# State-space scan of a decoder: which engine makes the C products, and when the next round is prepared

## The reference

```python
h = _rms(x, norm_w[i])
xz = jnp.einsum('bld,ed->ble', h, W_in[i])
xi, z = jnp.split(xz, 2, axis=-1)
xc = _silu(conv_b[i] + sum((xp[:, k:k + L, :] * conv_w[i][:, k] for k in range(dc))))
delta, Bm, Cm = jnp.split(jnp.einsum('bld,ed->ble', xc, W_x[i]), [rk, rk + n], axis=-1)
delta = jax.nn.softplus(jnp.einsum('blr,dr->bld', delta, W_dt[i]) + b_dt[i])
deltaA = jnp.exp(delta[..., None] * A)
BX = (delta * xc)[..., None] * Bm[:, :, None, :]
_, hs = jax.lax.associative_scan(combine, (deltaA, BX), axis=1)
y = jnp.einsum('bldn,bln->bld', hs, Cm) + D[i] * xc
x = x + jnp.einsum('bld,ed->ble', y * _silu(z), W_out[i])
```

## Time and profile before

| what | value |
|---|---|
| median of 3 runs | 1598.68 us (1598.49 to 1600.09) |
| the profiled execution: its time, its span | 1598.81 us, 1597.1 us |
| busy over the span: PE / DVE / ACT / POOL | 1211.0 / 1111.4 / 753.1 / 857.8 us |
| the selective state-space units on VectorE | from 423.95 us to about 1248 us |
| scans with the C product behind them (L1468) | 160, 1821 ns each |
| scans with the C product on GpSimd (L1472) | 96, 1808 ns each |
| C products on VectorE (L1470) / on GpSimd (L1409) | 160 of 991 ns / 48 of 3571 ns |
| mean granted TensorE clock | 0.864 |

### The profile page before, as it was taken

One profiled execution on the slowest core, in us unless ns is written; L12 is line 12 of the kernel. 1 busy time (PEld: TensorE's weight loads), 2 busy tenths in 40 slices (PEclk: granted clock), 3 DMA queues, 4 the chain that ended last, 5 costly groups with the idle time before them and its releaser, 6 DMA issues.

```text
span 1597.1 us, 17149 instructions
## 1 busy us (share of the span) xinstructions
PE 1211.0 (76%) x5882; PEld 697.4 (44%) x5882; DVE 1111.4 (70%) x1630; ACT 753.1 (47%) x1692; POOL 857.8 (54%) x744
## 2 busy tenths in 40 slices
PE   6688888774568778787886868877777777788765
PEld 3454554442234444444443435444343445545444
DVE  3766767753487987879878888797888245554448
ACT  1454544533465455554555545545543144444553
POOL 5500010010587797778977879779787234343413
PEclk9898999987778888888998979888988789898976
DMA  6000010000502304014040050220400300000000
GB/s 183 20 10 10 10 60 1 1 1 0 204 1 84 118 0 166 14 43 160 0 152 27 2 200 1 100 80 1 165 1 1 93 26 15 14 14 1 2 1 21
DMA packets 21028, 79.88 MB, mean 50 GB/s; under 512 B 4273, under 2 KB 7417, under 8 KB 19961
## 3 DMA queue, kind: packets, MB, share of 16 engines
q1 hardware_dynamic: 20942, 78.79, 14.1%
HBM read 77.55 MB, written 1.23 MB: 49 GB/s over the span
## 4 chain that ended last, share of the span: by engine, by line
DVE 32%; PE 31%; POOL 15%; ACT 11%; issue 9%; DMA 1%; SPq 0%; DVEq 0%; ACTq 0%; POOLq 0%
PE ps L484 29%; DVE ps L1468 9%; POOL arena L1409 6%; POOL arena L1398 6%; DVE arena L1472 4%; DVE arena L1470 4%; DVE hstat L867 3%; ACT arena L691 3%; ACT L479 2%; DVE arena L854 2%; ACT ps L1311 2%; PE ps L548 1%; DVE arena L919 1%; ACT arena L701 1%; DVE arena L911 1%
## 5 line engine op out<-in xcount | busy, mean ns | idle before, releaser
L484 PE MATMUL ps<-arena 128*32 128x100 f32 (+12 forms) x3188 | 539.4, 407 | 213.1 <-issue 54.1
L484 PEld LDWEIGHTS ps<-arena 128*32 128x32 f32 (+10 forms) x3188 | 273.1, 157 | 436.6 <-issue 219.8
L1398 POOL TENSOR_TENSOR arena<-arena 128x1600 f32<-128x1600 f32 x128 | 455.6, 3578 | 6.8 <-DMA arena<-bc_scratch 5.7
L484 PE MATMUL ps<-arena,ident 128*128 128x400 f32 x1024 | 397.1, 541 | 58.0 <-DVE arena L1470 41.6
L1311 ACT ACTIVATE ps<-arena 128x400 f32<-128x400 f32 x512 | 282.4, 587 | 294.1 <-DVE arena L1470 250.7
L1468 DVE TENSOR_TENSOR_SCAN ps<-ps,arena 128x800 f32<-128x800 f32 x160 | 291.4, 1821 | 108.2 <-ACT ps L1311 73.2
L484 PEld LDWEIGHTS ps<-arena,ident 128*128 128x128 f32 x1024 | 207.2, 206 | 238.5 <-issue 64.3
L1409 POOL TENSOR_TENSOR arena<-arena 128x1600 f32<-128x1600 f32 x48 | 171.4, 3571 | 136.7 <-DVE arena L1472 136.7
L691 ACT ACTIVATE arena<-ps,hstat 100x361 f32<-100x361 f32 x256 | 144.2, 565 | 193.1 <-DVE hstat L867 193.1
L1472 DVE TENSOR_TENSOR_SCAN arena<-ps,arena 128x800 f32<-128x800 f32 x96 | 169.5, 1808 | 37.4 <-POOL arena L1398 24.0
L459 POOL TENSOR_SCALAR stat<-stat 100x1 f32<-100x1 f32 (+1 forms) x44 | 8.9, 202 | 329.0 <-DVE stat L440 328.4
(11 more groups left out here) (163 smaller groups left out, 1018.1 us busy)
## 6 DMA issues: line engine op xcount, KB each, us to landing
arena<-bc_scratch SPq DMA_DIRECT2D x64, 800.0 KB, 5.6
arena<-in_ctxT SPq DMA_DIRECT2D x16, 361.0 KB, 3.0
arena<-in_w_in SPq DMA_DIRECT2D x4, 1024.0 KB, 8.2
arena<-in_expT SPq DMA_DIRECT2D x1, 2048.0 KB
arena<-in_w_out SPq DMA_DIRECT2D x4, 512.0 KB, 3.3
arena<-in_mask SPq DMA_DIRECT2D x8, 141.0 KB
wo<-in_L_Wo SPq DMA_DIRECT2D x2, 512.0 KB
arena<-in_xT SPq DMA_DIRECT2D x1, 800.0 KB
```

The lines of the kernel that those rows point to most:

```text
L484: return nc.tensor.matmul(outp, lhsT, rhs, start=first, stop=last)
L1398: nc.gpsimd.tensor_tensor(bx[:, unit % BX].rearrange("p (j t) -> p j t", j=SEGMENT), bbc[:, nq].rearrange("p (j t) -> p j t", j=SEGMENT), ...
```

## The change

The change edits two tables and two functions. `DVE_C` still has ten units of sixteen: 2, 10 leave, 3 and 7 come in, so that the last unit of each block (3, 7, 11, 15) has its C product on VectorE. In `AT`, the gated sums (`vY`) are issued two steps earlier, output product, residual and most pieces of the preparation one step earlier; D2 and D3 move from step 13 to 12, beside D0 and D1, and X2 and X3 from step 8 to 9. In `am_silu`, two of the four gates are read ahead of the large Silu. In `mam_pool`, the root comes behind the step's Bx and ahead of its C product.

```diff
-DVE_C = (0, 1, 2, 4, 6, 10, 11, 12, 14, 15)
+DVE_C = (0, 1, 3, 4, 6, 7, 11, 12, 14, 15)
...
-    "pO": 3,
-    "vR": 4,
+    "pO": 2,
+    "vR": 3,
...
-    "pX": (7, 7, 8, 8, 10, 10, 11, 11),
+    "pX": (7, 7, 9, 9, 10, 10, 11, 11),
...
-    "pD": (12, 12, 13, 13),
-    "aD": 13,
+    "pD": (12, 12, 12, 12),
+    "aD": 12,
...
-    "vY": (6, 10, 14, 18),
+    "vY": (4, 8, 12, 16),
...
+        def am_gate(act, m, g, c):
+
+            n = f"X{CD + c}"
+            p_full(act, m, n)
+            nc.scalar.activation(sz[:, g, c], ps[:, p_bank(m, n), 0:GT], ACT.Silu).then_inc(p_done(m, n), 1)
+
         def am_silu(act, m, g):
+            for c in (0, 1):
+                am_gate(act, m, g, c)
             for c in range(CD):
                 p_read(act, m, f"X{c}")
             nc.scalar.activation(xc[:, g], xc[:, g], ACT.Silu).then_inc(m_xc, 1)
-            for c in range(CD):
-                n = f"X{CD + c}"
-                p_full(act, m, n)
-                nc.scalar.activation(sz[:, g, c], ps[:, p_bank(m, n), 0:GT], ACT.Silu).then_inc(p_done(m, n), 1)
+            for c in (2, 3):
+                am_gate(act, m, g, c)
...
                     if m + 1 < ROUNDS:
-                        if u == AT["gN"]:
-                            gm_rstd(pool, m + 1)
...
                         gm_bx(pool, unit + 1)
+                    if m + 1 < ROUNDS and u == AT["gN"]:
+                        gm_rstd(pool, m + 1)
                     if not on_dve(u):
                         gm_c(pool, unit)
```

More of the change, by code:

```diff
@@ L94 @@
     "1FTc": 11,
-    "pO": 3,
-    "vR": 4,
+    "pO": 2,
+    "vR": 3,
     "aK": 3,
[L98 to L102, removed]
-    "pX": (7, 7, 8, 8, 10, 10, 11, 11),
-    "aC": (8, 8, 9, 9),
-    "vC": (8, 9),
-    "aS": 11,
+    "aQ": 4,
+    "gN": 5,
+    "aH": 5,
+    "pT": 6,
+    "aT": 6,
+    "pX": (7, 7, 9, 9, 10, 10, 11, 11),
+    "aC": (7, 7, 8, 8),
+    "vC": (7, 8),
+    "aS": 10,
     "pB": 11,
-    "aB": 12,
-    "pD": (12, 12, 13, 13),
-    "aD": 13,
+    "aB": 11,
+    "pD": (12, 12, 12, 12),
+    "aD": 12,
     "aA": 14,
     "gA": 15,
-    "gD": (14, 15, 16, 17),
-    "vY": (6, 10, 14, 18),
+    "gD": (13, 14, 15, 16),
+    "vY": (4, 8, 12, 16),
 }
```

## The result

| | before | changed |
|---|---|---|
| median | 1598.59 us (4 runs) | 1639.88 us (1635.05 to 1642.47, 4 runs) |
| ratio, 95% interval | | 1.0255 [1.0227, 1.0283], slower |
| profiled execution: time, span | 1598.81, 1597.1 us | 1642.47, 1640.7 us |
| VectorE busy over the span | 1111.4 us | 1109.9 us |

The forecast was 1623 us in a range of 1600 to 1650, slower with a chance of 0.86. Direction and places are right, the size is not: 41 us were lost where 24 were forecast.

The account below looks back on a forecast made before the run. VectorE, executing in order, was taken as the bound: its work plus waits. Waits of 20.4 us a period against 17.1 gave +3.3, seven times +23, with +0 to +1 elsewhere: 1598.8 + 24 = 1623 us, range 1600 to 1650.

Parts of the forecast that it names:

- (a): Output product and residual: issued a step earlier, the residual no longer waits; VectorE's wait of 2.6 us becomes 0.2.
- (b): Root behind Bx on GpSimd: waits before units 4 and 6 replace the one before unit 7; 2.7 us becomes 1.9.
- (c): Gated sum 1, now after unit 8: new wait for unit 7's reduction behind X2 and X3, 2.2 us.
- (d): Silu block on ScalarE: with two gates read first, VectorE's wait goes from 6.4 us to 5.8.
- (e): Gated sum 2, after unit 12: reductions stand on TensorE behind D2 and D3; wait goes from 4.46 us to 7.4.
- (f): Before unit 15: GpSimd's Bx comes late with only unit 14 beside it; new wait of 2.9 us.
- Rival 1: TensorE does not hold reductions back behind D2, gated sum 2 comes in time; 1581 us, faster; chance 0.07.
- Rival 3: No change: all terms at their lower ends, TensorE at full clock throughout; 1593 us; chance 0.10.
- Rival 2: Low clock at output product, gated sums 1 and 2 and Silu block: +10 us a period, 1669 us; chance 0.12.

Follow-up runs that it names:

- experiments 1 to 3: From the changed kernel: D2 and D3 at step 14, 1600.62 us; gated sum 2 back behind unit 14, 1600.71 us; D2 and D3 at step 13, 1602.43 us.
- experiment 1: The changed kernel with D2 and D3 moved from TensorE's step 12 to 14, behind unit 11's reduction: 1600.62 us.
- Experiment 5: The changed kernel with 18 extra unused matmuls behind D1, in TensorE's 4.9 us stop ahead of D2: 1615.01 us.
- experiment 7: The changed kernel with the root ahead of the step's Bx in GpSimd's program, as before: 1651.68 us.
- experiment 3: The changed kernel with D2 and D3 in TensorE's step 13, between the reductions of units 10 and 11: 1602.43 us.

## Why the prediction was right, and where it was not

The waits over 0.25 us, as means of the seven periods:

| step | before | forecast | measured after |
|---|---|---|---|
| (a) output product, residual, unit 5 | 1.7 (2.6 in the earlier trace rows) | 0.2 | 0.0 |
| (b) units 4 and 6 (before: unit 7) | 2.7 | 1.9 | 2.2 |
| (c) gated sum 1 | 0 | 2.2 | 2.4 |
| (d) Silu block | 5.5 (6.44 in the earlier trace rows) | 5.8 | 6.2 |
| (e) Softplus block, gated sum 2 | 4.9 (4.46 in the earlier trace rows) | 7.4 | 8.7 |
| (f) unit 15 | 0 | 2.9 | 2.9 |
| other places | 1.4 | 0 | 0 |
| sum, of unrounded values | 16.2 | 20.4 | 22.4 |

**Right.** The bound: VectorE's busy time did not move, the waits did. Every place with a wait over 0.5 us was named with its releaser, and the four new ones are there. That the sum for block 2 stands in TensorE's queue behind D2 is shown by experiments 1 to 3. Rival 1 is out, in the changed kernel and in experiment 1: TensorE did not take the reductions ahead of the waiting D2, and when they were put ahead of it the wait was gone. Rival 3 is out.

**Wrong in size, in two steps.** First, term (e) was 1.3 short. I had charged 2.2 us of low clock, from the middle of two rows, and all of it to the reductions. Experiment 5 prices it at 3.2: both deltas and a part of the reductions ran at 1.2 GHz. The other 0.3 is in the chain itself, 5.5 at the full clock where I had 5.2. My row of 1.61 for D2 and D3 was taken after a stop of 1.83 us; in the changed kernel the stop is 4.91 and the same four records take 3.03. The forecast named that stop ("some 4 us") and still used the duration from after the short one. Terms (b), (c) and (d) are short by 0.2 to 0.4 each.

In term (d) the shortfall is the clock too, and here the stop does not even differ. In all seven periods X4 and X5 come after a stop of 3.59 or 3.60. They took 2.95 in two, 4.51 or 4.65 in two and 5.55 to 5.70 in three, and the wait before unit 11 was 5.64, 5.77 and 6.68 to 6.84. This is read from the rows; no run was made to test it. Two of these periods, with a granted clock of 0.53 and of 1.00:

```profile
697.90 5.55 PE L484 MATMUL ps<-arena 128*128 128x400 f32 x8 [3.60 <-DVE arena L1455]
807.27 2.95 PE L484 MATMUL ps<-arena 128*128 128x400 f32 x8 [3.59 <-DVE arena L1455]
```

Second, the comparison was uneven. I set my list of 20.4 against 17.1, which is all of VectorE's idle time, small gaps included, though my own list of before came to 16.2. The places over 0.25 us make only 16.2 of it, and the small gaps stay (0.9 before, 0.8 after). Like against like, the forecast would have been +4.2 a period instead of +3.3, some 6 us more. Over seven periods that is 6 us, term (e) 9 and the other terms together 5: 20 us, which is what the profiled execution of 1642.5 us lies above the forecast; the median of 1639.9 lies 17 above it.

Rival 2, the low clock everywhere, happened in full at one place of four in the changed kernel, gated sum 2, and in part at a second, the Silu block, where it cost about 0.5 a period and not the 2.7 of the rival. At gated sum 1 it did not happen in the changed kernel, but it did in five periods of experiment 7.

## What to carry to other kernels

A step that is moved earlier in one engine's program also moves ahead of what stands behind it; list for each moved instruction what it waits for, and who waits for those that it now holds up. A reader put earlier than its producer can be ready holds its whole engine, so move the producer's queue first and the reader after it. Compare waits place by place with the same threshold on both sides, and take a duration from rows whose engine had stood still at least as long as it will in the new order. Take several such rows, and forecast a range: the same stop was followed here by different durations.

## What the runs showed of the hardware

Stops of TensorE of a few us cost more than themselves. After 4.91 us D2 and D3 took 3.03 instead of 1.61; after 3.22 us X2 and X3 took 4.65, after 2.07 us 2.95. The length of a stop alone does not settle it: after 3.59 us the same eight records took anything from 2.95 to 5.70, and after 2.03 us D2 and D3 took 1.61 in six periods of experiment 3 and 3.03 in one. What decides between them these runs leave open. Filling the first stop with 4.27 us of useless matmuls took 24 us off. I had expected the effect, but not that moving five GpSimd instructions of 0.2 us would reach the time through it.
